# Graph blocks on one core: a new order of the four engines' slots, the weights' hi/lo splits moved

## Time and profile before

| | us |
|---|---|
| median of three runs | 1386.93 (1386.03 to 1387.05) |
| the profiled execution, its own time | 1388.81 |
| its span, first to last instruction | 1387.0 |
| PE busy | 1358.5 (98%) |
| DVE busy | 1227.9 (89%) |
| ACT busy | 912.3 (66%) |
| POOL busy | 124.5 (9%) |
| granted TensorE clock, mean of the span | 0.99 |
| share of the chain that ended last that is PE | 95% |
| DMA, mean over the span | 35 GB/s |

### The profile page before, as it was taken

The page is one execution under the profiler, slowest core; times in us unless marked ns, Lnnn a source line. Parts: engine busy times, 40 slices in busy tenths (PEclk is TensorE's granted clock), DMA queues, the critical chain, the costliest instruction groups (busy, mean ns, idle before and its releaser), DMA issues.

```text
span 1387.0 us, 30079 instructions
## 1 busy us (share of the span) xinstructions
PE 1358.5 (98%) x11005; PEld 1196.8 (86%) x11005; DVE 1227.9 (89%) x3820; ACT 912.3 (66%) x2444; POOL 124.5 (9%) x265
## 2 busy tenths in 40 slices
PE   6999999999999999999999999999999999999996
PEld 6888889888889888889888889888889888889884
DVE  5689999999999999999999999999999999999985
ACT  4466776666776666776666777666776666776663
POOL 0000101101001101101101101101101101101101
PEclk9899999999999999999999999999999999999998
DMA  5111001111011111001111011111001111001000
GB/s 180 33 32 32 11 30 40 40 41 40 11 31 40 40 40 41 12 30 40 41 40 40 10 32 40 40 41 40 13 29 40 40 40 41 14 28 40 9 9 23
DMA packets 51313, 48.99 MB, mean 35 GB/s; under 512 B 7904, under 2 KB 50656, under 8 KB 51168
## 3 DMA queue, kind: packets, MB, share of 16 engines
q1 hardware_dynamic: 51168, 47.08, 10.7%
HBM read 38.68 MB, written 8.39 MB: 34 GB/s over the span
## 4 chain that ended last, share of the span: by engine, by line
PE 95%; ACT 2%; DVE 1%; issue 0%; DMA 0%; SPq 0%; POOL 0%; POOLq 0%; DVEq 0%
PE psum L922 63%; PE psum L936 12%; PE psum L1127 9%; PE psum L1104 8%; PE psum L1179 1%; PE psum L1182 1%; PE psum L1192 1%; PE psum L1201 0%; DMA w_raw<-in_L_gnn_W 0%; PE psum L943 0%; ACT work L454 0%; DVE work L767 0%; ACT wqkv_h L320 0%; ACT w_h L320 0%; DVE bn L571 0%
## 5 line engine op out<-in xcount | busy, mean ns | idle before, releaser
L454 ACT ACTIVATE work<-work,shift 128x256 f32<-128x256 f32 x512 | 253.9, 500 | 44.9 <-DVE shift L748 44.9
L767 DVE SCALAR_TENSOR_TENSOR work<-work,rsum,extra 128x256 f32<-128x256 f32 x512 | 221.2, 479 | 1.2
L748 DVE CUSTOM_DVE_ANT_0 work<-psum,minus_big 128x256 f32<-128x256 f32 x512 | 192.7, 419 | 16.5 <-PE psum L1104 15.4
L320 ACT ACTIVATE work<-psum 128x512 f32<-128x512 f32 x256 | 144.5, 594 | 9.7 <-PE psum L936 9.7
L922 PE MATMUL psum<-x2T_h,wqkv_h 128*128 128x256 f32 x512 | 148.7, 290 | 1.3 <-DVE x2T_l L555 1.2
L922 PE MATMUL psum<-x2T_l,wqkv_h 128*128 128x256 f32 x512 | 142.2, 278 | 0.0
L922 PE MATMUL psum<-x2T_h,wqkv_l 128*128 128x256 f32 x512 | 142.1, 278 | 0.0
L936 PE MATMUL psum<-ident,work 128*128 128x128 f32 x1024 | 139.7, 274 | 0.7 <-DVE work L767 0.7
L302 POOL TENSOR_TENSOR mv<-mv,eps 128x2 f32<-128x2 f32 x128 | 25.6, 200 | 1248.4 <-DVE mv L592 1248.4
L1127 PE MATMUL psum<-work,v_sb 128*64 128x256 f32 x1024 | 131.9, 389 | 0.9 <-ACT work L320 0.9
L320 ACT ACTIVATE sup_h<-psum 128x512 fp32r<-128x512 f32 x128 | 76.4, 597 | 74.0 <-PE psum L922 74.0
(11 more groups left out here) (130 smaller groups left out, 3806.2 us busy)
## 6 DMA issues: line engine op xcount, KB each, us to landing
xT_sb<-in_xT SPq DMA_DIRECT2D x32, 256.0 KB, 2.8
adjT_sb<-in_adjT SPq DMA_DIRECT2D x32, 256.0 KB, 3.1
adj_sb<-in_adj SPq DMA_DIRECT2D x32, 256.0 KB, 4.2
x_sb<-in_x SPq DMA_DIRECT2D x32, 256.0 KB, 4.4
out<-y_sb SPq DMA_DIRECT2D x32, 256.0 KB, 2.2
work<-in_L_gnn_W_qkv SPq DMA_DIRECT2D x1, 1536.0 KB, 9.8
mask_row<-in_nodemask SPq DMA_DIRECT2D x32, 32.0 KB, 4.1
w_raw<-in_L_gnn_W SPq DMA_DIRECT2D x3, 256.0 KB, 5.4
```

The source lines that it names most:

```text
L320: return nc.scalar.activation(dst, src, ACT.Copy, scale=scale)
L454: last = nc.scalar.activation(prob[:, p % 2, i, h], prob[:, p % 2, i, h], ACT.Exp, bias=shift[:, p % 2, h, i:i + 1], scale=-1.0, accum_out ...
L748: last = V_.tensor_tensor_reduce(out=prob[:, p % 2, i, h], in0=bank(SCORES[p] + h)[:, i * N:(i + 1) * N], in1=minus_big[:, g % 2, i], scal ...
L767: last = V_.scalar_tensor_tensor(out=prob[:, p % 2, i, h], in0=prob[:, p % 2, i, h], scalar=rsum[:, p % 2, h, i:i + 1], in1=extra[:, g % 2 ...
```

## The change

All four `slot` functions get a new order. PE: scores of pairs 0 and 1 stand together, scores 2, the transposes of pair 0 and the transpose of x1 and scores 3 stand together, the attention products of pairs 0 and 1 stand together with `gate_row` behind; pair 2's product follows the transposes of pair 3, pair 3's stands between `support(2)` and `gcn_out`; `support0` of the next graph is cut, its HI part ahead of `project_out`; x3's transpose stands between `qk` 0 and 1. DVE: the norm of x2 and that of x3 follow each other directly. ACT: `adj_hi` stands ahead of the first `exps`, `exps` of pair 3 behind `hidden(0)`. New PSUM banks, and with them other extra waits. The splits of the weights at graph 0 move: w123 behind `adj_hi` instead of `sup0_hi`, wqkv behind the first two `sup_hi`, w_out and w3 behind the third. `keep_busy`: 44 instead of 40, 21 instead of 18, and 12 more ahead of `support(1)` and `support(2)` of graph 0. No product, split, exponential or DMA is added or left out.

```diff
 SUP0 = 4
-SELF = 5
-AGG = 6
-X1T = 3
-GCN = 1
-X2T = 7
-VALUES = 0
-Y = 0
-X3T = 7
-PROJ3 = 4
-ADJK = 3
-GATE_ROW = 6
-GATE_COL = 6
-SUP = (4, 3, 3)
-HID = (6, 4)
-QK = (3, 6, 1, 6)
-SCORES = (2, 6, 4, 4)
-PROBT = ((2, 7), (7, 2), (1, 6), (6, 2))
-PV = (0, 5, 7, 3)
+SELF = 1
+AGG = 4
+X1T = 6
+GCN = 3
+X2T = 5
+VALUES = 6
+Y = 7
+X3T = 3
+PROJ3 = 6
+ADJK = 0
+GATE_ROW = 0
+GATE_COL = 2
+SUP = (7, 7, 5)
+HID = (3, 3)
+QK = (0, 2, 0, 1)
+SCORES = (4, 2, 2, 4)
+PROBT = ((4, 7), (1, 6), (5, 2), (2, 7))
+PV = (6, 1, 4, 6)
 MASK = 0
 
...
 BIAS_DMAS = 4
-FIRST, LAST = -2, G + 4
...
     def slot(s):
-        norm_rstd(0, s - 1)
-        norm_rstd(1, s - 1)
-        norm_rstd(3, s - 4)
-        norm_rstd(2, s - 2)
+        norm_rstd(2, s - 6)
+        norm_rstd(3, s - 7)
+        norm_rstd(0, s - 4)
+        norm_rstd(1, s - 4)
...
     def adj_hi(g):
...
+        if g == 0:
+            act.wait_ge(dma_w123, 16 * 3)
+            for i in range(3):
+                weight_hi(w123[0][:, i], w123_raw[:, i])
...
     def adj_exp(g):
...
+        reuse(act, dve_extra, once(g - 1))
...
     def sup0_hi(g):
...
-        if g == 0:
-            act.wait_ge(dma_w123, 16 * 3)
-            for i in range(3):
-                weight_hi(w123[0][:, i], w123_raw[:, i])
...
         copy(fT[0][:, :, :], halves(bank(X1T))).then_inc(act_x1T, 1)
-        if g == 0:
-            act.wait_ge(dma_wqkv, 16)
-            for k in range(FT):
-                weight_hi(wqkv[0][:, k].rearrange("p i (h d) -> p i h d", d=D),
-                          wqkv_raw[:, k].rearrange("p (h i d) -> p i h d", i=3, d=D))
 
     def sup_hi(layer, g):
         if not live(g):
             return
         act.wait_ge(pe_sup[layer], once(g))
         copy(sup[0][:, :, :], halves(bank(SUP[layer]))).then_inc(act_sup[layer], 1)
-        if g == 0 and layer == 0:
+        if g == 0 and layer < 2:
+            act.wait_ge(dma_wqkv, 16)
+            weight_hi(wqkv[0][:, layer].rearrange("p i (h d) -> p i h d", d=D),
+                      wqkv_raw[:, layer].rearrange("p (h i d) -> p i h d", i=3, d=D))
+        if g == 0 and layer == 2:
             act.wait_ge(dma_wout, 16)
...
     def slot(s):
...
+        exps(s - 7, 2, 0)
+        sup_hi(0, s - 6)
+        probs_t(s - 7, 1, 0)
+        probs_t(s - 7, 1, 1)
+        exps(s - 7, 2, 1)
+        hidden(0, s - 6)
+        hidden_hi(0, s - 6)
+        exps(s - 7, 3, 0)
+        exps(s - 7, 3, 1)
+        sup_hi(1, s - 6)
+        out_hi(s - 7, 0)
+        probs_t(s - 7, 2, 0)
+        probs_t(s - 7, 2, 1)
+        x_hi(s - 5)
+        out_hi(s - 7, 1)
+        hidden(1, s - 6)
+        hidden_hi(1, s - 6)
+        probs_t(s - 7, 3, 0)
+        probs_t(s - 7, 3, 1)
+        gate_exps(s - 8)
+        out_hi(s - 7, 2)
+        sup_hi(2, s - 6)
+        out_hi(s - 7, 3)
+        x2_hi(s - 6)
+        gate_column(s - 8)
+        degrees(s - 5)
+        mask_bias(s - 6)
+        x3_hi(s - 7)
+        adj_exp(s - 5)
+        sup0_hi(s - 5)
+        qk_hi(s - 6, 0)
+        qk_hi(s - 6, 1)
+        tail_qkv(s - 7)
+        adj_hi(s - 5)
+        exps(s - 6, 0, 0)
+        exps(s - 6, 0, 1)
+        self_copy(s - 5)
+        exps(s - 6, 1, 0)
+        exps(s - 6, 1, 1)
+        qk_hi(s - 6, 2)
+        qk_hi(s - 6, 3)
+        values(s - 6)
+        probs_t(s - 6, 0, 0)
+        probs_t(s - 6, 0, 1)
+        x1_hi(s - 5)
...
         lo(adjT[1][:, g % 2], adjT_sb[:, g % 2], adjT[0][:, g % 2]).then_inc(dve_adjT, 1)
+        if g == 0:
+            weight_lo(w123[1][:, 0], w123_raw[:, 0], w123[0][:, 0], W1)
...
-        if g == 0:
-            weight_lo(w123[1][:, 0], w123_raw[:, 0], w123[0][:, 0], W1)
...
-        if g == 0:
-            wqkv_lo(0)
...
-        if g == 0 and layer == 0:
-            wqkv_lo(1)
+        if g == 0 and layer < 2:
+            wqkv_lo(layer)
+        if g == 0 and layer == 2:
+            weight_lo(wout[1][:, :, :], wout_raw[:, :, :], wout[0][:, :, :], W_OUT)
+            weight_lo(w3[1][:, :, :], w3_raw[:, :, :], w3[0][:, :, :], W_LAST)
...
-        if g == 0 and layer == 0:
-            weight_lo(wout[1][:, :, :], wout_raw[:, :, :], wout[0][:, :, :], W_OUT)
-            weight_lo(w3[1][:, :, :], w3_raw[:, :, :], w3[0][:, :, :], W_LAST)
...
-        if p == 2 and i == 0:
+        if p in (2, 3) and i == 0:
             dve.wait_ge(pe_probT, nth2(g, p - 2, 1))
...
     def slot(s):
...
+        sup_lo(0, s - 4)
+        scores(s - 5, 3, 0)
+        scores(s - 5, 3, 1)
+        recip_sums(s - 5, 2)
+        probs(s - 5, 2, 0)
+        probs(s - 5, 2, 1)
+        hidden_lo(0, s - 4)
+        recip_sums(s - 5, 3)
+        probs(s - 5, 3, 0)
+        sup_lo(1, s - 4)
+        probs(s - 5, 3, 1)
+        x2_bias(s - 5)
+        x_lo(s - 3)
+        gate_maximum(s - 6)
+        hidden_lo(1, s - 4)
+        x1_bias(s - 4)
+        out_lo(s - 5, 0)
+        out_lo(s - 5, 1)
+        out_lo(s - 5, 2)
+        gate_probs(s - 6)
+        sup_lo(2, s - 4)
+        out_lo(s - 5, 3)
+        norm_apply(3, s - 7)
+        gcn_out(s - 4)
+        norm_stats(1, s - 4)
+        norm_mean(1, s - 4)
+        norm_apply(1, s - 4)
+        attention_out(s - 5)
+        norm_stats(2, s - 5)
+        norm_mean(2, s - 5)
+        x2_lo(s - 4)
+        tail_out(s - 6)
+        norm_apply(2, s - 5)
+        norm_stats(3, s - 6)
+        adj_extra(s - 4)
+        degrees(s - 3)
+        x3_lo(s - 5)
+        adj_sum(s - 3)
+        sup0_lo(s - 3)
+        qk_lo(s - 4, 0)
+        qk_lo(s - 4, 1)
+        tail_k(s - 5)
+        scores(s - 4, 0, 0)
+        scores(s - 4, 0, 1)
+        norm_mean(3, s - 6)
+        scores(s - 4, 1, 0)
+        adj_lo(s - 3)
+        tail_gate(s - 5)
+        scores(s - 4, 1, 1)
+        recip_sums(s - 4, 0)
+        probs(s - 4, 0, 0)
+        aggregate(s - 3)
+        relu_residual(s - 3)
+        recip_sums(s - 4, 1)
+        norm_stats(0, s - 3)
+        norm_mean(0, s - 3)
+        qk_lo(s - 4, 2)
+        probs(s - 4, 0, 1)
+        norm_apply(0, s - 3)
+        qk_lo(s - 4, 3)
+        probs(s - 4, 1, 0)
+        scores(s - 4, 2, 0)
+        x1_lo(s - 3)
+        probs(s - 4, 1, 1)
+        scores(s - 4, 2, 1)
...
     def aggregate(g, part):
...
             pe.wait_ge(act_adjT, once(g))
+            pe.wait_ge(act_sup0, once(g))
             pe.wait_ge(dve_adjT, once(g))
-            pe.wait_ge(act_sup0, once(g))
         else:
...
     def x1_transpose(g):
         if g == 0:
-            keep_busy(7, 40)
+            keep_busy(7, 44)
         pe.wait_ge(dve_x[0], once(g))
...
     def support(layer, g, part):
+            if g == 0 and layer:
+                keep_busy(5, 12)
             weights(g, W1 + layer)
             if layer == 0:
                 pe.wait_ge(act_x1T, once(g))
-                reuse(pe, dve_scores, nth2(g - 1, 2, 1))
             if layer == 1:
             if layer == 2:
...
     def hidden(layer, g, part):
             if layer == 0:
-                reuse(pe, dve_qk, nth(g - 1, 3))
-            if layer == 1:
-                reuse(pe, dve_scores, nth2(g - 1, 3, 1))
+                reuse(pe, dve_scores, nth2(g - 1, 2, 1))
         else:
...
     def x2_transpose(g):
         if g == 0:
-            keep_busy(7, 30)
+            keep_busy(2, 30)
         pe.wait_ge(dve_x[1], once(g))
...
     def qk(g, p):
         weights(g, W_QKV + 1)
         pe.wait_ge(dve_x2T, once(g))
-        if p == 1:
-            reuse(pe, act_gate_col, once(g - 2))
+        if p == 2:
+            reuse(pe, dve_gate, once(g - 1))
         if p == 3:
-            pe.wait_ge(dve_agg, once(g + 1))
+            pe.wait_ge(act_self, once(g + 1))
...
     def scores(g, p):
         pe.wait_ge(dve_qk, nth(g, p))
-        if p in (0, 1):
+        if p == 1:
             pe.wait_ge(act_qk, nth(g, p))
-        if p == 2:
-            pe.wait_ge(act_self, once(g + 1))
+        if p == 3:
+            pe.wait_ge(act_probT, nth2(g, p - 3, 0))
+        if p == 0:
+            pe.wait_ge(act_sup0, once(g + 1))
...
     def probs_t(g, p, h):
         pe.wait_ge(dve_prob, nth2(g, p, h))
-        if p == 1 and h == 0:
+        if p == 3 and h == 0:
             pe.wait_ge(act_probT, nth2(g, p - 1, 1))
+        if p == 0 and h == 1:
+            pe.wait_ge(act_v, once(g))
...
     def attend(g, p):
         pe.wait_ge(act_v, once(g))
-        if p == 1:
-            pe.wait_ge(dve_scores, nth2(g, p + 2, 1))
+        if p == 0:
+            pe.wait_ge(act_probT, nth2(g, p + 1, 1))
+        if p == 3:
+            pe.wait_ge(dve_oT, nth(g, p - 3))
...
     def x3_transpose(g):
         if g == G - 1:
-            keep_busy(7, 30)
+            keep_busy(6, 30)
         pe.wait_ge(dve_x[2], once(g))
...
     def tail_project(g, part):
             weights(g, W_LAST)
             pe.wait_ge(act_x3T, once(g))
-            pe.wait_ge(dve_sup0, once(g + 2))
         else:
...
     def gate_row(g):
         pe.wait_ge(dve_gate, once(g))
-        pe.wait_ge(act_probT, nth2(g + 1, 3, 0))
         for t in range(NT):
...
```

(90 more changed lines are left out.)

125 lines of the change are left out of this document (1 added, 124 removed).

## The result

The changed kernel takes 1374.1 us (median of four runs, 1373.0 to 1375.1) beside 1386.5 of the kernel before: ratio 0.9908, 95% interval 0.9896 to 0.9920. It gains 12.4 us where 18.9 were forecast. The time lies in the forecast's own range.

The account below looks back on a forecast made before the run. PE, busy 98% of the span, was taken as the bound, with time moving only by neighbour costs, short waits and the start. 0.42 us less a period times 31 is 13, the start 6: 1386.9 - 13 - 6 = 1368, range 1362 to 1376.

Parts of the forecast that it names:

- The neighbours: PE's steady state: what one instruction costs behind another; the new order saves 0.26 us a period.
- the waits: PE's short waits in a period: 0.36 us go, about 0.2 come in their place, 0.1 each at x3 and scores 0.
- the start: Filling before the steady state: weight splits moved off the path and a clock that stays high gain 3 to 7.4, taken as 6.
- The new groups: PE's regrouped work: scores 0 and 1 together 1.81 us, products 0 and 1 2.07, pair 3's transposes with product 2 2.08.
- Product 3 and `gate_row` at 0, bounds -0.10 to +0.15: PE: separating these two, and C and x2's transpose changing places, taken as no cost because no row shows these neighbours.
- x3: PE's transpose of x3: 3.9 us of work against 3.9 of cover, a wait of 0.1, bounds 0 and 0.5.
- Scores 0: PE's scores 0, due at 8.0, waits for `qk_lo(0)`, ready at 8.1: a wait of 0.1, bounds 0 and 0.4.
- the probabilities of pair 0 are due only at `probs_t`, 9 us later: `exps(0)` now waits for `adj_hi`, hence K, and comes about 2 us later behind its scores; held to be covered.
- At `recip_sums(3)`: DVE waits there for `exps(3, 1)` behind `hidden(0)`: about 1 us idle, with nothing on PE due for 2.
- the splits: Start: wqkv's split moved takes about 1.2 us off the path; w_out's and w3's low parts ahead of `gcn_out` cost 1.3.
- DVE as the bound: Rival: two of DVE's unfilled waits double, the period becomes 42.2 and the kernel slower, 1399 us; chance 0.1.
- The rule on tiling modes: Skill page: a mode change drains TensorE; 13 changes against 12 give 0.19 a period instead of 0.26, total 1370.

Follow-up runs that it names:

- scores_apart: Changed kernel with the tail's product with K put between scores 0 and scores 1 on PE: 1398.0 us, 1.0074 of the kernel before.
- gate_between: Changed kernel with `gate_row` between attention products 0 and 1 on PE instead of behind them: 1383.0 us, 0.9971 of the kernel before.
- adj_three_mean: Changed kernel with the transposed adjacency's high half in three buffers and `norm_mean(3)` ahead of `tail_k` on DVE: 1368.4 us, 0.9850 of the kernel before.
- x3_extra: Changed kernel with x3 in two buffers and DVE's order `adj_extra`, `norm_apply(2)`, `tail_out`: 1371.4 us, 0.9873 of the kernel before.
- x3_two: Changed kernel with x3 in two buffers and DVE's order `degrees`, `norm_apply(2)`, `tail_out`, `adj_extra`: 1388.0 us, 1.0007 of the kernel before.
- adj_three: Changed kernel with the transposed adjacency's high half in three buffers, so `adj_hi` need not wait for K: 1369.5 us, 0.9878 of the kernel before.
- bias_first: Changed kernel with DVE's `x2_bias` ahead of `recip_sums(3)` and `sup_lo(1)` ahead of `probs(3, 0)`: 1382.6 us, 0.9970 of the kernel before.
- row_early: Changed kernel with `norm_mean(3)` ahead of `tail_k` on DVE and pair 0's first `exps` ahead of `adj_hi` on ACT: 1379.6 us, 0.9943 of the kernel before.

## Why the forecast was right, and where it was not

- *The total*: in the range, and partly by luck. The neighbours brought some 0.15 us a period more than forecast, the waits cost some 0.3 more, and the start gave less; the first two are opposite errors.
- *The new groups*: right. Scores 0 and 1 last 1.62 (1.80 with 0.08 of entry and 0.10 of leaving, the latter as in scores_apart), products 0 and 1 1.87, the eight transposes and product 2 0.96 + 1.02 (730.18, 731.14, and 732.16 where F follows); four transposes alone 0.43. scores_apart and gate_between show that a kind's neighbours have a price, 0.29 and 0.33 for splitting a pair where the forecast had 0.37, and the forecast's main argument with it.
- *Product 3 and `gate_row` at 0, bounds -0.10 to +0.15*: outside the bounds. Product 3 and G together cost 749.29 - 747.27 - 0.59 = 1.43 in the kernel before (below). Now product 3 alone costs 734.96 - 733.17 - 0.59 = 1.20, and products 0 and 1 with G 726.43 - 723.65 - 0.59 = 2.19, 0.12 more than the 2.07 without it: -0.11. G ahead of a product holds PE 0.31, ahead of F 0.14. C and the transpose of x2 cost 0.84 before and 0.79 now: -0.16 in all. Without its waits (0.18 at x3, the 0.20 that adj_three_mean gives back, 0.10 at `hidden(1)`) the new order would take, as an estimate, 41.33 - 0.48 = 40.85, 0.15 under the forecast's 41.00. The neighbours brought more than forecast, the waits took it.

```profile
747.27 0.64 PE L922 MATMUL psum<-sup_l,adjT_h 128*128 128x256 f32 x4
747.75 0.38 PE L1192 MATMUL psum<-ident,gate 128*1 128x128 f32 x2
748.06 1.08 PE L1127 MATMUL psum<-work,v_sb 128*64 128x256 f32 x8
...
749.29 0.28 PE L922 MATMUL psum<-wout_l,oT_h 128*128 128x256 f32 x1
```

- *The waits in their place*: too low, 0.2 forecast, about 0.5 found, and at the places held to be safe.
  - x3: forecast 0.1, measured 0.18. that `x2_lo` and `tail_out` stand "between mean and apply, in POOL's time" is only partly so: POOL's root ends at 701.79 (701.10 + 0.69), `norm_apply(2)` starts at 702.22 behind `tail_out`. x3_extra and x3_two, in which it no longer stands there, have no wait at x3.
  - Scores 0: forecast 0.1, measured 0.
  - "the probabilities of pair 0 are due only at `probs_t`, 9 us later": the step that failed. The consumer named was the wrong one. On DVE, in the order written, the reciprocal of pair 0 stands ahead of `aggregate`, the sums of x1 and `qk_lo(2)`, and what is late is scores 2. adj_three shows it: with ACT no longer held by K, the period is 0.14 shorter.
  - At `recip_sums(3)` "DVE idles about 1 us, with nothing on PE due for 2": it idles 0.84, and `sup_lo(1)` behind it is 0.10 late for `hidden(1)`. bias_first shows both that this was the cause and that reordering here gives no gain.
- *Start*: forecast 6, 3.7 on the medians together with the end (2.9 with the start's hunks alone). The first `aggregate` comes 2.5 us earlier (14.21 to 11.75, forecast 2.7) and x2's first transpose 6.9 (47.86 to 40.92, forecast 6), but these are against an execution of before that is 1.9 us above its median, and the 4.5 us of slow products were read from it too. The clock held, as thought, but not for the twelve transposes. The other term that was mis-sized is the splits: "about 1.2 off the path", and 1.3 for w_out's and w3's low parts, where the chain shows 6.4 us of splits still on the path.
- *DVE as the bound*: the rival did not come, at a period of 41.33 it has 41.33 - 38.4 = 2.9 us of room. But x3_two and bias_first, with a few DVE steps in other places, are slower than the changed kernel by 13.7 and 8.6, and x3_two loses the whole gain: the rival's mechanism was one reordering away.
- The rule on tiling modes gave 1370 by a smaller gain of the neighbours. It came nearer in the sum and not by its reason: the neighbours brought more than forecast, not less. At the 0.15 a change that the two versions give, 13 changes against 12 would be worth 0.15 a period, and the neighbours brought about 0.4 (41.62 - 0.36 before, 40.85 now); where the rest comes from beyond the groups priced above is open.

## What to carry to other kernels

Where one engine is 98% busy, price a new order by starts of neighbouring groups; that part of a forecast can be right to a few hundredths where a row shows the same neighbours, and was off by 0.16 where none did. For each instruction that gets a new wait, do not ask when its own result is due, but go down the in-order queue of its consumer and ask for the first result behind it that is due at once. Moving a step of a full queue mostly moved the wait here, and often made it larger (bias_first, x3_two, row_early); taking the cause away (a buffer more) or filling a wait that is already there keeps the gain.
